# Two-layer decoder with routed expert layers: the expert's second product with a split inner width of 128 + 48

## The reference

```
logits = x @ gate.T                          # 8 experts
w, idx = top_k(softmax(logits), 2)
for each expert e of a token (2 of 8), and for the shared expert(s):
    h = x @ w1[e]                            # 256 -> 352 = 2 x 176
    y = (silu(h[:, :176]) * h[:, 176:]) @ w2[e]   # 176 -> 256
    out += weight * y                        # the shared expert's weight is 1
```

## Time and profile before

| | us |
|---|---|
| median of 3 runs (lowest, highest) | 877.12 (874.18, 885.82) |
| the profiled execution | 875.9 |
| its span, first to last instruction | 874.1 |
| PE busy with products / with weight loads | 676.2 (77%) / 497.0 (57%) |
| DVE / ACT / POOL busy | 567.1 (65%) / 382.9 (44%) / 173.6 (20%) |
| mean granted clock of TensorE | 0.888 of 2.4 GHz |
| L1680, transposes of `act`, 168 times, mean 286 ns | busy 34.1, idle before them 21.4 |

### The profile page before, as it was taken

How to read it: one execution, slowest core, us unless ns; L and a number is a source line. 1 busy time by engine, 2 the same in 40 slices (tenths; PEclk the granted TensorE clock), 3 DMA queues, 4 the chain that set the end, 5 groups by cost and what they waited for, 6 DMA issues and landing times. The chain is left out here.

```text
span 874.1 us, 16937 instructions
## 1 busy us (share of the span) xinstructions
PE 676.2 (77%) x6016; PEld 497.0 (57%) x6016; DVE 567.1 (65%) x1326; ACT 382.9 (44%) x816; POOL 173.6 (20%) x193
## 2 busy tenths in 40 slices
PE   3657778898768899776787788965578777689997
PEld 2334443464667788664465565544255554578996
DVE  5666654356675456675888898865866655665455
ACT  1024343302255355874575565541144345554553
POOL 5100000121400331016131121211511102203113
PEclk9689996999899899987799898986789796889999
DMA  8700000042112351014000000000033000114433
GB/s 298 257 2 2 1 2 2 0 157 113 48 43 68 127 156 39 18 42 108 2 6 6 6 7 1 12 1 1 0 117 117 23 37 16 53 37 140 139 116 109
DMA packets 39069, 53.09 MB, mean 61 GB/s; under 512 B 9874, under 2 KB 33170, under 8 KB 38558
## 3 DMA queue, kind: packets, MB, share of 16 engines
q1 hardware_dynamic: 35918, 43.62, 15.2%
q0 software_dynamic: 3072, 8.39, 3.1%
HBM read 37.97 MB, written 17.04 MB: 63 GB/s over the span
## 5 line engine op out<-in xcount | busy, mean ns | idle before, releaser
L1143 ACT ACTIVATE s_mega<-bank 128x512 f32<-128x512 f32 x96 | 56.7, 597 | 104.0 <-PE bank L1513 56.2
L1946 DVE TENSOR_REDUCE s_mega<-bank 128x2 f32<-128x512 f32 (+1 forms) x96 | 64.5, 686 | 37.3 <-PE bank L1484 21.1
L2087 DVE TENSOR_TENSOR s_mega<-bank,s_mega 128x176 f32<-128x176 f32 x84 | 28.4, 339 | 78.7 <-ACT s_mega L1183 78.6
L2149 DVE SCALAR_TENSOR_TENSOR s_mega<-s_mega,s_convw 128x256 f32<-128x256 f32 x144 | 67.9, 512 | 1.8 <-ACT s_mega L1245 0.8
L1333 ACT ACTIVATE s_mega<-bank 128x512 f32<-128x512 f32 x64 | 37.5, 602 | 37.5 <-PE bank L1780 37.5
L996 POOL DMA_INDIRECT xd<-s_xn,s_pos x32 | 34.1, 1065 | 94.8 <-issue 94.8
L1183 ACT ACTIVATE s_mega<-bank 128x176 f32<-128x176 f32 x84 | 26.8, 320 | 56.9 <-PE bank L1670 56.7
L945 POOL TENSOR_TENSOR s_rstd<-s_ve,s_mhalf 128x2 f32<-128x2 f32 x24 | 16.8, 699 | 171.6 <-DVE s_ve L1863 171.5
L1680 PE MATMUL bank<-s_ident,s_mega 128*88 128x128 f32 x168 | 34.1, 286 | 21.4 <-DVE s_mega L2087 21.4
L1480 PE MATMUL bank<-s_masks,s_identb 128*128 128x512 bf16 x64 | 29.3, 458 | 26.1 <-DVE s_mega L1946 26.0
L2220 DVE TENSOR_TENSOR s_mega<-s_mega 128x512 f32<-128x512 f32 x64 | 46.8, 735 | 2.4 <-ACT s_mega L1333 2.1
(11 more groups left out here) (276 smaller groups left out, 1928.1 us busy)
## 6 DMA issues: line engine op xcount, KB each, us to landing
s_mega<-xd SPq DMA_DIRECT2D x60, 128.0 KB, 2.1
yd<-s_mega SPq DMA_DIRECT2D x60, 128.0 KB, 1.7
s_wrawF<-in_wF SPq DMA_DIRECT2D x10, 608.0 KB, 6.0
s_wrawC<-in_wC SPq DMA_DIRECT2D x9, 608.0 KB, 10.0
xd<-in_zeros SPq DMA_DIRECT2D x2, 1920.0 KB, 17.4
s_mega<-in_win SPq DMA_DIRECT2D x1, 2112.0 KB, 10.2
s_mega<-in_hots SPq DMA_DIRECT2D x2, 704.0 KB
s_x<-in_x SPq DMA_DIRECT2D x4, 256.0 KB, 5.2
```

The source lines that it names most:

```text
L1143: a.activation(PT[:, p % NPT, :], AR[n % 3][:, :], ACT.Exp).then_inc(a_read, 1)
L1946: v.tensor_reduce(nM[:, q, h0:h0 + heads], V[n % 2][:, :].rearrange("p (h k) -> p h k", h=heads), AX.X, ALU.max, negate=True).then_inc(v_r ...
L2149: ins = v.scalar_tensor_tensor(o, raw[:, m % NRAW, h, KS - 1 - k:KS - 1 - k + L], convw[:, ct, KS - 1 - k:KS - k], o, ALU.mult, ALU.add)
```

## The change

The inner width 176 is cut into 128 + 48 (`FR` = 48) and no longer into 88 + 88. VectorE writes the product `act` 256 columns wide: columns 0 to 127 the first 128, then the other 48 twice, at 128 and at 192 (one instruction that reads its operands twice), with zeros between them, written once at the start of the stage ("switch"). The two transposes are 128 wide, so the 48 stand in rows 0 to 47 and again in rows 64 to 111 of the second half of `HB`. ScalarE copies all of it to `ah`. VectorE makes the low part of the first half in `al`, and of the second half only in rows 64 to 127, in place in `ah`: so that operand holds the high part of the 48 above and their low part below. The weights of the 48 are laid out twice, to match. The second layer is then five products of 128 rows: high weight with first high and first low, low weight with first high, high weight with the joint operand, low weight with the joint operand. (The last also takes in low weight x low activation of the 48, which was left out before.) `sg` and `act` of C move to other places in memory.

```diff
--- before.py
+++ after.py
@@ -64,7 +64,7 @@
 HALF = TOK // 2
 TH = HALF // P
 GU = 2 * FE
-FH = FE // 2
+FR = FE - P
 WU = KD * GU + 2 * D
 NBK = (2 * HALF + NE * (P - 1)) // P
 SHARED = {"C": 1, "F": 2}
@@ -653,12 +653,14 @@
         work = {}
         for s_, base in WORK.items():
             g0 = base + NGB * D
-            small = ARENA + 1280 if s_ == "C" else base + 5120
+            small = 5132 if s_ == "C" else base + 5120
+            inner = ARENA + 1280 if s_ == "C" else small + 2 * FE
             work[s_] = {
                 "gathered": words(base, NGB, D), "rows": words(g0, NR, D), "yb": words(g0 + NR * D, NYB, D),
                 **{name: [a[:, D * n:D * (n + 1)] for n in range(2)] for name, a in split[s_].items()},
-                "sg": words(small, 2, FE), "act": words(small + 2 * FE, 2, FE)}
-            assert g0 + 14 * D <= (WIN if s_ == "C" else HI["F"])
+                "sg": words(small, 2, FE), "act": words(inner, 2, 2 * P)}
+            assert g0 + 14 * D <= (WIN if s_ == "C" else HI["F"]) and inner + 4 * P <= (ARENA + 1984 if s_ == "C" else HI["F"])
+        assert 5132 + 2 * FE <= HI["C"]
         assert 18 * D <= AUX + 3328
         def sems(names):
             return [sem(n) for n in names.split()]
@@ -1186,7 +1188,7 @@
                     act.wait_ge(bat_full, n + 1)
                     if n >= 2:
                         act.wait_ge(dn_full, n - 1)
-                    a.copy(work[s]["ah"][n % 2][0:FH, :], HB[n % 2][0:FH, 0:2 * P]).then_inc(ah_ready, 1)
+                    a.copy(work[s]["ah"][n % 2], HB[n % 2][:, 0:2 * P]).then_inc(ah_ready, 1)
                 elif kind == "bx":
                     f = info[s, i]
                     if not f["new_x"]:
@@ -1677,7 +1679,7 @@
                         pe.wait_ge(ah_ready, n - 1)
                         pe.wait_ge(al_ready, n - 1)
                     for h in range(2):
-                        ins = tr(HB[n % 2][0:FH, h * P:(h + 1) * P], work[s]["act"][n % 2][:, h * FH:(h + 1) * FH], ident[:, :])
+                        ins = tr(HB[n % 2][:, h * P:(h + 1) * P], work[s]["act"][n % 2][:, h * P:(h + 1) * P], ident[:, :])
                     ins.then_inc(bat_full, 1)
                 elif kind == "dn":
                     f = info[s, i]
@@ -1687,10 +1689,11 @@
                     if f["new_y"] and f["y"] >= 2:
                         pe.wait_ge(yb_ready, f["y"] - 1)
                     at_unit = offsets[n % 4]
-                    ah_, al_ = (work[s][name][n % 2].rearrange("p (k t) -> p k t", k=2) for name in ("ah", "al"))
-                    parts = [("h", ah_, 0), ("h", al_, 0), ("h", ah_, 1), ("h", al_, 1), ("l", ah_, 0), ("l", ah_, 1)]
+                    first_h, first_l, rest_ = work[s]["ah"][n % 2][:, 0:P], work[s]["al"][n % 2][:, 0:P], work[s]["ah"][n % 2][:, P:2 * P]
+
+                    parts = [("h", first_h, 0), ("h", first_l, 0), ("l", first_h, 0), ("h", rest_, 1), ("l", rest_, 1)]
                     for p_, (w_, a_, k) in enumerate(parts):
-                        ins = mm(Y[f["y"] % 2][:, 0:D], a_[0:FH, k, :], w2[s][w_][0:FH, bass.ds(at_unit + KD * GU + k * D, D)],
+                        ins = mm(Y[f["y"] % 2][:, 0:D], a_, w2[s][w_][:, bass.ds(at_unit + KD * GU + k * D, D)],
                                  start=(f["new_y"] and p_ == 0), stop=(f["end_y"] and p_ == len(parts) - 1), skip_group_check=True)
                     ins.then_inc(dn_full, 1)
                 elif kind == "din":
@@ -2084,13 +2087,20 @@
                     dve.wait_ge(sg_ready, n + 1)
                     if n >= 2:
                         dve.wait_ge(bat_full, n - 1)
-                    v.tensor_tensor(work[s]["act"][n % 2], G[n % 2][:, FE:GU], work[s]["sg"][n % 2], ALU.mult
-                                    ).then_inc(act_ready, 1)
+                    a_, sg_ = work[s]["act"][n % 2], work[s]["sg"][n % 2]
+                    v.tensor_tensor(a_[:, 0:P], G[n % 2][:, FE:FE + P], sg_[:, 0:P], ALU.mult)
+
+                    v.tensor_tensor(a_[:, P:2 * P].rearrange("p (r w) -> p r w", r=2)[:, :, 0:FR],
+                                    G[n % 2][:, FE + P:GU].unsqueeze(1).to_broadcast([P, 2, FR]),
+                                    sg_[:, P:FE].unsqueeze(1).to_broadcast([P, 2, FR]), ALU.mult).then_inc(act_ready, 1)
                 elif kind == "bat":
                     n = info[s, i]["n"]
                     dve.wait_ge(ah_ready, n + 1)
-                    v.tensor_tensor(work[s]["al"][n % 2][0:FH, :], HB[n % 2][0:FH, 0:2 * P],
-                                    work[s]["ah"][n % 2][0:FH, :].bitcast(F32), ALU.subtract).then_inc(al_ready, 1)
+                    ah_ = work[s]["ah"][n % 2]
+                    v.tensor_tensor(work[s]["al"][n % 2][:, 0:P], HB[n % 2][:, 0:P], ah_[:, 0:P].bitcast(F32), ALU.subtract)
+
+                    v.tensor_tensor(ah_[HS:P, P:2 * P], HB[n % 2][HS:P, P:2 * P], ah_[HS:P, P:2 * P].bitcast(F32), ALU.subtract
+                                    ).then_inc(al_ready, 1)
                 elif kind == "bx":
                     f = info[s, i]
                     if not f["new_x"]:
@@ -2123,6 +2133,12 @@
                         dve.wait_ge(x_moved, move_at[s, i] - 1)
                     v.scalar_tensor_tensor(x[:, t, :], work[s]["gathered"][k % NGB], wts[:, hf, m // 2, m % 2:m % 2 + 1],
                                            x[:, t, :], ALU.mult, ALU.add).then_inc(x_moved, 1)
+                elif kind == "switch" and s in "CF":
+
+                    if first[s]:
+                        dve.wait_ge(*previous(s))
+                    for n in range(2):
+                        v.memset(work[s]["act"][n][:, P:2 * P].rearrange("p (r w) -> p r w", r=2)[:, :, FR:], 0.0)
                 elif kind == "d_init":
                     before_d(dve)
                     dve.wait_ge(mix_in, 96)
@@ -2290,7 +2306,8 @@
     def unit(gate, up, down):
 
         gu = np.concatenate([gate, up], 1).reshape(KD, P, GU).transpose(1, 0, 2).reshape(P, KD * GU)
-        dn = np.pad(down.reshape(2, FH, D), ((0, 0), (0, P - FH), (0, 0))).transpose(1, 0, 2).reshape(P, 2 * D)
+        rest = np.pad(down[P:], ((0, HS - FR), (0, 0)))
+        dn = np.concatenate([down[:P], np.concatenate([rest, rest])], 1)
         return np.concatenate([gu, dn], 1)
 
     w1, w2 = f["L0_ffn_w1"], f["L0_ffn_w2"]
```

## The result

The changed kernel takes 890.02 us (median of 4 runs, 885.98 to 892.57) against 877.18 for the kernel before: ratio 1.0103 [1.0059, 1.0148]. Measured again later beside other kernels it took 892.39 against 878.86, ratio 1.0167 [1.0120, 1.0214]. So it is slower, by 13 us as the medians go and by 9 and 15 as the two ratios go, where 878.0 had been forecast, 0.8 over before, with a range that ended at 886.

A forecast was written before the change was run, and what follows sets the result against it. PE's sequencer was taken to bound routed blocks, the array shared ones, VectorE the first blocks of either mixture stage. VectorE's +5.1 and PE's -3.2 gave +1.9 on 875.9 us: 878, range 869 to 886.

The forecast's parts named there:

- VectorE's price: VectorE's split gating product and low part, per block: +0.12 and +0.27, together +0.39 us, lower end +0.21.
- Rival D: VectorE's half-row low part overlaps its neighbours after all: +0.21 per block, 875.4 us in all; chance 0.15.
- It hides: Routed or shared blocks of the even stretch: VectorE's added 0.39 us costs nothing, each result being used one block later.
- the sequencer has no time left: Routed blocks: PE's sequencer, not the array, sets the period; waits, a 444 ns read and register work fill it.
- 13 x 0.39: VectorE's added time counts only where PE waits for the gating product: 12 waits, plus 3, minus 2; +5.1 us.
- rival B: Slower by the clock: longer waits make PE resume at 1.2 GHz more often; 887 us, chance 0.16.
- seven more such steps: Rival B's condition: it decides from seven more steps at 1.2 GHz on, each 1.3 us longer.
- PE's gain of 3.2: One second-layer product less per block: 1.0 in routed, 1.4 in array-held, 0.8 in 1.2 GHz steps; -3.2 us.
- 0.04 per routed block: PE's sequencer time saved by one load and product less; 25 blocks give 1.0 us.
- two after 848: Two array-held steps after 848 us whose gain of 0.12 us each reaches the end.
- Rival A: The array sets the time in all blocks, and one product less saves 9.9 us: 866.0 us; chance 0.10.
- C: As a rival: 128-row products take longer, or five cost what six do; 881 us, chance 0.07.

The follow-up runs named there:

- f1: Changed kernel with VectorE's second low part as a full 128-row instruction writing the joint operand, no half rows; 882.5 us, ratio 1.0020 to the kernel before.
- e4: Changed kernel with only the low part joined into one 128x256 instruction (joint operand's low part left out), gating product still split; 876.8 us, ratio 0.9963 to before.
- g3: Changed kernel without the bounds check of the expert's place after PE's sequencer reads it; 883.7 us, ratio 1.0057 to the kernel before.
- f3: Kernel before the change, without the bounds check of the expert's place; 875.0 us, ratio 0.9951 to the kernel before.
- f2: Changed kernel with the weights of the 48 joined instead of the activations, one low-part instruction, five products; 878.4 us, ratio 0.9997 to before.
- f4: f2 without the bounds check of the expert's place; 873.0 us, ratio 0.9914 to the kernel before.
- e1: Changed kernel with a sixth second-layer product (low weight x first high a second time); 894.4 us, ratio 1.0144 to the kernel before.
- e2: Changed kernel with VectorE's gating product and low part each joined as before (joint operand's low part left out), five products kept; 877.8 us, ratio 0.9997.
- e3: Changed kernel with VectorE making the next input's low part ahead of the low part of act; 886.6 us, ratio 1.0084 to the kernel before.

## Why the prediction was wrong, step by step

**VectorE's price was right.** One routed block of the changed kernel, VectorE in order of time:

```profile
833.38 0.29 DVE L2091 TENSOR_TENSOR s_mega<-bank,s_mega 128x128 f32<-128x128 f32 x1 [0.84 <-ACT s_mega L1185]
...
833.59 0.25 DVE L2093 TENSOR_TENSOR s_mega<-bank,s_mega 128x96 f32<-128x96 f32 x1
833.75 0.28 DVE L2100 TENSOR_TENSOR s_alF<-bank,s_ahF 128x128 fp32r<-128x128 f32 x1
...
834.04 0.29 DVE L2102 TENSOR_TENSOR s_ahF<-bank,s_ahF 64x128 fp32r<-64x128 f32 x1
...
834.37 0.42 DVE L2111 TENSOR_TENSOR s_xlF<-bank,s_xhF 128x256 fp32r<-128x256 f32 x1
```

Gating 0.37 (forecast 0.38), low part 834.37 - 833.75 = 0.62 (forecast 0.60): +0.40 per block against +0.39. The half-row instruction starts 0.01 after the end of the one before it, and the next one 0.04 after its end, where full-row neighbours (833.59 to 833.75) overlap by 0.09. The rule of the Trainium skill, "VectorE: DVE Perf Modes", section "Two Vector instructions with no wait between them", foretold just this, and f1, whose operands all start at row 0, shows the other side of it: 0.45. Rival D (it overlaps) is out.

**"It hides" in the even stretch was wrong.** VectorE is idle 37% of it even now (31.60 of 50.35 us busy), and each result is used a block later, as the prediction said. But the low part of the next input is used sooner: its bank is single, so PE's transposes of the input after it wait for that low part, and PE's sequencer stands there with everything else behind it. The sequencer's records in one routed block of the changed kernel (durations, first and last start): the wait of the transposes of `act`, of those of the input, of the second layer, and the next block's first wait:

```profile
L1680 PEldq EVENT_SEMAPHORE  x1: 51/51/51, 836.9 to 836.9; - x1
...
L1647 PEldq EVENT_SEMAPHORE  x1: 51/51/51, 837.4 to 837.4; - x1
...
L1690 PEldq EVENT_SEMAPHORE  x1: 51/51/51, 837.5 to 837.5; - x1
...
L1660 PEldq EVENT_SEMAPHORE  x1: 51/51/51, 838.1 to 838.1; - x1
```

The same four in the kernel before:

```profile
L1678 PEldq EVENT_SEMAPHORE  x1: 51/51/51, 814.1 to 814.1; - x1
...
L1645 PEldq EVENT_SEMAPHORE  x1: 51/51/51, 814.2 to 814.2; - x1
...
L1688 PEldq EVENT_SEMAPHORE  x1: 51/51/51, 814.3 to 814.3; - x1
...
L1658 PEldq EVENT_SEMAPHORE  x1: 51/51/51, 814.9 to 814.9; - x1
```

VectorE in the changed kernel, the low part of the input ahead of that wait:

```profile
836.89 0.42 DVE L2111 TENSOR_TENSOR s_xlF<-bank,s_xhF 128x256 fp32r<-128x256 f32 x1
```

Before, the sequencer passes from the first record to the second in 0.1 us; now it takes 0.5, until VectorE's low part ends (836.89 + 0.42 = 837.31). In 17 of the 20 records of L1647 in these steps it is so: they start 0.04 us after VectorE's low part ends, later than the 0.13 us at which one record can follow another; before, not one of 20 does, in f1 11, in e4 7. The record's own 51 ns hide the wait: it is seen only in the distance to the record ahead of it. I had read "the sequencer has no time left" as "nothing else can be late". The loop is: first layer, `silu`, four instructions of VectorE, low part of the input, then the wait, the second layer, the read of the place and the next first layer but one. From the first layer at 834.28 to that at 839.04 it takes 4.76 us, 2.38 per block. With 0.40 less it would be 4.36, 2.18 per block, below the 2.30 that the sequencer needs; so there was, by this estimate, slack of 2 x 2.30 - 4.36 = 0.24 us in two blocks, and 0.40 was over it. e4's 0.12 fits in (2.27); f1's 0.24 is at the edge (2.35); g3 confirms the loop from the sequencer's side. PE's idle time before the first layer in these 21 blocks (loads and products, us and times), in the kernel before:

```profile
  issue: 2.2, 8
```

and in the changed one:

```profile
  issue: 11.0, 32
```

The gap that the prediction wanted 0.08 longer grew by far more.

**"13 x 0.39" was too little for the early parts, and rival B has a share in it.** The early parts lost 7.9 and not 5.1. Take the eighth first layer of C (L1672), PE in order of time in the changed kernel:

```profile
264.70 0.41 PE L1650 MATMUL bank<-s_ident,s_mega 128*128 128x128 f32 x2 [0.62 <-DVE s_xlC L2111]
...
266.86 0.49 PE L1672 MATMUL bank<-s_whC,s_xlC 128*128 x1
267.15 0.49 PE L1672 MATMUL bank<-s_whC,s_xhC 128*128 x1
```

The table of stretches, ahead of this first layer and from it on (the sixth value, ahead of the DMA share, is the granted clock):

```profile
262.00:265.60 3.60, 1.34 (x9) 1.08 (x10) 3.51 (x14) 1.06 (x3) 0.00 (x0) 1.00 0.00 0
266.40:268.75 2.35, 2.35 (x10) 2.28 (x10) 0.00 (x0) 0.77 (x2) 0.00 (x0) 0.50 0.28 93
```

The same place in f1, where PE's wait is 0.19 us shorter:

```profile
264.39 0.41 PE L1651 MATMUL bank<-s_ident,s_mega 128*128 128x128 f32 x2 [0.43 <-DVE s_xlC L2112]
...
266.36 0.32 PE L1673 MATMUL bank<-s_whC,s_xlC 128*128 x1
266.52 0.32 PE L1673 MATMUL bank<-s_whC,s_xhC 128*128 x1
```

and its stretches:

```profile
262.00:265.31 3.31, 1.37 (x9) 1.11 (x10) 3.28 (x14) 0.94 (x3) 0.00 (x0) 1.00 0.00 0
266.10:268.42 2.32, 2.26 (x16) 2.04 (x16) 0.71 (x4) 1.32 (x5) 0.00 (x0) 1.00 0.28 96
```

Ahead of it either kernel is at full clock and PE works 1.34 of 3.60 us here, 1.37 of 3.31 there. Then the clock is at 0.50 in the changed kernel, which is 1.2 GHz, and products stand 0.29 apart; in f1 it stays at 2.4 GHz and they stand 0.16 apart. The step to the ninth first layer takes 3.41 us and not 2.30 (before) or 2.32 (f1). It does so (3.06 to 3.52) in all six profiles whose early blocks have the half-row pair, and in one of the eight without (f3). Two steps of F are long at a lower clock too: the one to its eighth block, 5.94 at 0.50, against 4.22 at 0.86 before and 4.53 at 0.94 in f1, and the one to its 16th, 3.42 at 0.58, against 2.27 at 1.00 before. Over f1 and before these three are 1.1 + 1.4 + 1.15 = 3.7 us. So B's mechanism is there, and its condition was wrong: "seven more such steps" were not needed, and "most of the added time is short beside waits of 2.7 to 3.8 us" was the wrong argument, since at the first place the clock falls or stays with the 0.17 us per block by which f1 differs from the changed kernel. In F the pair does not decide alone: f2 and f4, without it, take 6.57 (clock 0.80) and 5.69 (0.50) to the eighth block, f2 also 3.57 (0.55) to the 16th, and e1, with it, 5.04 (0.81) and 2.50 (1.00).

Nor does the clock carry the whole loss. The two early stretches of e1:

```profile
241.94:307.56 65.62, 48.98 (x304) 43.95 (x304) 41.69 (x151) 30.40 (x78) 9.23 (x11) 0.89 0.23 72
760.15:812.54 52.39, 40.93 (x247) 35.84 (x248) 37.71 (x128) 27.02 (x63) 5.79 (x7) 0.90 0.16 49
```

They lose 7.7 us at 0.89 and 0.90, where the kernel before has 0.92 and 0.88; the sixth product may be 1.3 of that, as e2 with five is 1.3 under before. And f3, without the pair and the check, loses only 1.2 at 0.81 and 0.86. The 4.2 us that are left of the 7.9 would be VectorE's time of eleven blocks, near the prediction's count (12 waits, +3, -2); but by that count e4 and f1 would have lost 1.3 and 2.6 here, and they lost 0.0 and 0.5. So it is shown that the half-row pair makes the early loss, and that the loss is out of proportion; how it divides between the clock and the waits stays open. No run held the clock and changed the waits alone.

**PE's gain of 3.2 did not come.** The 0.04 per routed block was misread from the rows. The 0.5 us there belongs to the four register operations, which start 0.11 to 0.14 us apart in the blocks shown (before: 814.41, 814.55, 814.67, 814.78), whether one or two pairs of load and product lie between them; a pair adds nothing. From the second layer's wait to the next block's first wait the sequencer takes 0.6 us with five products (837.5 to 838.1) and with six (814.3 to 814.9). With VectorE's work as before the 21 steps of e2 take 48.07 us against 48.30, 0.01 each (0.06 by the median, which one profile of either kernel can't tell from nothing). The "two after 848" are there (0.12 each), but the gathers end the kernel anyway, as the prediction said of the other six. In total e2, all gain and no cost of VectorE, is 0.3 us faster [-3.9, +3.3]. The two figures of the Trainium skill weighed there ("TensorE: Matmul & The Clock Gate", section "Wait — 56ns, not 53.3ns?") would give, as an estimate, 0.6 to 1.6 us in 25 blocks; no run here can tell these from nothing.

**The account.** Over the kernel before, in the second profile, which has D and E like it: early parts +8.1, the step between them and the 21 +0.7, 21 routed steps +2.0, the rest of C +1.2, D and E -0.6, last eight -1.0, start and end together +1.2: 11.6, the difference of the spans (885.7 - 874.1). The prediction had +5.1 - 3.2 = +1.9. In its terms: the early 5.1 came out as 8.1, the even stretch, put at nothing, cost 2.0, and of the 3.2 only the 1.0 of the last eight is seen. Rival A fell with e2. Of C the first half fell, as 128 rows cost what 88 do; its second half, that five products cost the six, held where the sequencer sets the step and fell among the shared blocks (0.12 each).

## What to carry to other kernels

A result "used one block later" hides only if every reader of it is followed to the next single buffer; the slack of such a loop (here 0.24 us in two blocks) is the figure to set the added time against. A small addition is priced by what it tips, here a loop past its slack and at some places the clock to its lower level, and not by its own length. Before a product is saved, look at what its engine's sequencer does besides: dropping a check was worth 0.5%, the product nothing that could be measured. And a mean over equal steps is worth a look at its longest step.

## What the runs showed of the hardware

- A sequencer's wait can be missing from the record's duration: 51 ns at L1647 in every one of 20 routed blocks, while its start lay up to 0.7 us late (at 856.9, the record before it at 856.1); at L1690 in e3 the wait is in the duration (51/176/387 ns).
- Where addresses come from a register, one pair of load and product more or less did not change the time that PE's sequencer takes for a layer (0.6 us with five and with six); one register operation less did (0.47 us in f2, which has three and not four).
- Stages that were not touched vary by 5.8 us (367.1 to 372.9) from one profile to the next, which is half of the difference looked for here, so a single profile's total can't carry it; stretches cut at the same instruction can.
